# An LSTM scan on one core: every gate computed with the weights as the loaded operand

## What is computed

```python
def step(carry, xw_t):
    prev_h, prev_c = carry
    a = xw_t + prev_h @ Wh
    i = sigmoid(a[:, :H]); f = sigmoid(a[:, H:2*H]); o = sigmoid(a[:, 2*H:3*H]); g = tanh(a[:, 3*H:])
    next_c = f * prev_c + i * g
    next_h = o * tanh(next_c)
    return (next_h, next_c), next_h
# xW = x @ Wx + b, x is (2, 1024, 256); h0 = cond (2, 256), c0 = 0, H = 256
x = x + scan(step, (h0, c0), xW)          # 1024 steps, one after the other
x = x + ((x * (y * s)) @ weight) * rsqrt((y * s)**2 @ weight**2 + 1e-8)   # y = cond, s = 1/16
```

## Time and profile before

| | us |
|---|---|
| median of three runs (1942.17 to 1943.12) | 1943.04 |
| the profiled execution | 1940.92 |
| its span, from the first to the last instruction | 1939.1 |
| TensorE busy with matmuls / with loads | 1739.9 / 1577.4 |
| VectorE busy | 1263.6 |
| ScalarE busy | 886.4 |
| GpSimd busy | 258.1 |
| TensorE clock granted, mean share of 2.4 GHz | 0.996 |

### The profile page before, as it was taken

One profiled execution on the slowest core, in us unless ns is written; L12 is line 12 of the kernel. 1 busy time (PEld: TensorE's weight loads), 2 busy tenths in 40 slices (PEclk: granted clock), 3 DMA queues, 4 the chain that ended last, 5 costly groups with the idle time before them and its releaser, 6 DMA issues.

```text
span 1939.1 us, 303170 instructions
## 1 busy us (share of the span) xinstructions
PE 1739.9 (90%) x135928; PEld 1577.4 (81%) x135928; DVE 1263.6 (65%) x12825; ACT 886.4 (46%) x6148; POOL 258.1 (13%) x1295
## 2 busy tenths in 40 slices
PE   7989899999989898989999999889898989999998
PEld 7888888888888888888888888888888888888886
DVE  4666666666666666666666666666666666666665
ACT  2444444444444444444444444444444444444443
POOL 1111111111111111111111111111111111111110
PEclk8999999999999999999999999999999999999999
DMA  3000000000000000000000000000000000000001
GB/s 94 0 0 0 0 0 0 0 0 0 0 0 0 0 0 0 0 0 0 0 0 0 0 0 0 0 0 0 0 0 0 0 0 0 0 0 0 0 0 43
DMA packets 4444, 6.68 MB, mean 3 GB/s; under 512 B 1106, under 2 KB 2900, under 8 KB 4436
## 3 DMA queue, kind: packets, MB, share of 16 engines
q1 hardware_dynamic: 3872, 5.51, 0.9%
q10 hardware_dynamic: 564, 1.05, 0.2%
HBM read 4.46 MB, written 2.10 MB: 3 GB/s over the span
## 4 chain that ended last, share of the span: by engine, by line
PE 72%; ACT 15%; DVE 7%; issue 5%; DMA 0%; ACTq 0%
PE pA L221 24%; PE pS L235 15%; PE pB L235 14%; ACT tanhc L192 8%; ACT ogate L190 7%; DVE hst L384 7%; PE pA L228 6%; PE pA L207 6%; PE pA L201 6%; PE pA L322 1%; DMA bias_col<-in_bC_dram 0%; PE pB L213 0%; PE pS L313 0%; ACTq L173 0%; DVE ores L399 0%
## 5 line engine op out<-in xcount | busy, mean ns | idle before, releaser
L221 PE MATMUL pA<-wh_sb,hst 128*4 128x64 f32 (+2 forms) x24576 | 654.0, 220 | 180.0 <-DVE hst L384 177.9
L185 ACT ACTIVATE gates<-pB 128x8 f32<-128x8 f32 x2048 | 351.4, 184 | 1014.6 <-DVE pB L368 1006.1
L368 DVE STREAM_TRANSPOSE pB<-pA 128x64 f32<-128x64 f32 x2048 | 444.9, 263 | 449.4 <-PE pA L221 449.3
L221 PEld LDWEIGHTS pA<-wh_sb,hst 128*4 128x4 f32 (+2 forms) x24576 | 395.2, 87 | 295.4 <-DVE hst L384 292.8
L235 PE MATMUL pS<-hst,wh_sb 128*32 128x2 f32 x32768 | 509.7, 177 | 1.5 <-issue 1.5
L372 DVE CUSTOM_DVE_ANT_1 junk<-gates 128x4 f32<-128x4 f32 x4096 | 424.6, 160 | 113.8
L235 PE MATMUL pB<-hst,wh_sb 128*32 128x2 f32 x32768 | 465.0, 174 | 0.0
L235 PEld LDWEIGHTS pB<-hst,wh_sb 128*32 128x32 f32 x32768 | 430.6, 110 | 0.0
L143 POOL TENSOR_TENSOR xh<-xh,hst 128x4 f32 (+1 forms) x1024 | 206.9, 202 | 1652.1 <-DVE hst L384 1652.1
L235 PEld LDWEIGHTS pS<-hst,wh_sb 128*32 128x32 f32 x32768 | 423.9, 108 | 1.6 <-issue 1.6
L228 PE MATMUL pA<-wh_sb,hst 128*4 128x32 f32 (+3 forms) x16384 | 423.1, 193 | 0.0
(11 more groups left out here) (41 smaller groups left out, 295.5 us busy)
## 6 DMA issues: line engine op xcount, KB each, us to landing
outT_dram<-ores SPq DMA_DIRECT2D x8, 256.0 KB, 2.5
xh<-in_xT_dram SPq DMA_DIRECT2D x6, 320.0 KB
wh_sb<-in_Wh_dram ACTq DMA_DIRECT2D x1, 1024.0 KB, 8.1
wx_sb<-in_Wx_dram SPq DMA_DIRECT2D x1, 1024.0 KB, 7.6
w_sb<-in_w_dram SPq DMA_DIRECT2D x1, 256.0 KB, 6.7
xh<-in_xT_dram SPq DMA_DIRECT2D x2, 64.0 KB, 8.2
bias_sb<-in_bT_dram ACTq DMA_DIRECT2D x2, 1.0 KB
condT<-in_condT_dram ACTq DMA_DIRECT2D x1, 2.0 KB, 7.8
```

What stands on the lines that cost most here:

```text
L185: act.activation(gates[:, j, :, 0:2 * PAIR].rearrange("p b (q a) -> p a q b", a=PAIR), pB[:, j, :, 0:PAIR * Q].rearrange("p a (q r) -> p a ...
L221: last = pe.matmul(pA[j][c * Q:c * Q + M, 0:PAIR * Q].rearrange("p (g u) -> p g u", u=Q), hst[:, k, lo:lo + M], two(wh_sb[:, k, :], c, j, ...
L368: dve.transpose(pT[j][:, 0:PAIR * Q], pA[j][:, 0:PAIR * Q]).then_inc(turned_and_fsum_ready[j], 1)
```

## The change

- `turned`, `turned_one`, `two`, `fill_bias` and `fill_x` go, and with them the transposes of L368 and the bank `pA`. All four gates are computed with a 128x32 tile of the weights as the stationary operand (`add_h`): 48 matmuls for i, f and g and 16 for o in each step.
- h streams as `WIDE` = 16 columns, of which 14 are zeros: `hst` is laid out so that a window of 16 columns at `WIDE * t` has h at columns 2t and 2t+1. Each matmul adds to all 16 columns of its sum.
- i, f and g of one half lie side by side in one bank (`cells[j]`), and the sigmoid reads them there once TensorE is done with the half.
- All x sums go to banks of their own (`xcells`, `xouts`). `sum_x_cells(0)` (24 matmuls) runs in the first step of a body, `sum_x_cells(1)` (24) in the second, `sum_x_outs` (16) in the third. DVE carries them over with the bias in three additions, all in the first step of a body.
- `FILL` puts 1, 1, 2 and 1 fillers at the ends of the four steps.
- Step s of a body works on column pair t = (s + 3) % 4 where it was (s + 1) % 4, and `xp` is filled four time steps further ahead (`bodies`, POOL).

The diff, cut to its core:

```diff
-    TURNED = (I_, G_)
-    STILL = (F_, O_)
+    CELL_GATES = (I_, F_, G_)
+    NG = len(CELL_GATES)
     T = 4
     ROWS = T * B
+    WIDE = 16
+    LEAD = T - 1
     NBODY = SEQ // T
     CELL = 8
     AT_I, AT_F, AT_G, AT_HALF, AT_C = 0, 1, 2, 4, 5
     WARM = 32
-    AT_X = 256
+    FILL = (1, 1, 2, 1)
...
+        hst = sb("hst", [P, K, T * WIDE])
...
-        pA = [ctx.enter_context(nc.psum_tensor(f"pA{j}", [P, 512], F32)) for j in range(K)]
-        pB = ctx.enter_context(nc.psum_tensor("pB", [P, K, PAIR, 512], F32))
+        pG = ctx.enter_context(nc.psum_tensor("pG", [P, K, 512], F32))
         pS = ctx.enter_context(nc.psum_tensor("pS", [P, K, 512], F32))
-
-        pT = [pB[:, j, 0, :] for j in range(K)]
-        sums = [pB[:, j, 1, :] for j in range(K)] + [pS[:, j, :] for j in range(K)]
-        pD, pX, pO = pS[:, 0, :], pT[0][:, AT_X:AT_X + PAIR * K * ROWS], pA
+        pX = ctx.enter_context(nc.psum_tensor("pX", [P, K + 1, 512], F32))
+        pF = ctx.enter_context(nc.psum_tensor("pF", [P, 512], F32))
+        cells = [pG[:, j, 0:NG * WIDE].rearrange("p (n r) -> p n r", r=WIDE) for j in range(K)]
+        outs = [pS[:, j, 0:WIDE] for j in range(K)]
+        xcells = [pX[:, j, 0:NG * ROWS].rearrange("p (n r) -> p n r", r=ROWS) for j in range(K)]
+        xouts = pX[:, K, 0:K * ROWS].rearrange("p (j r) -> p j r", r=ROWS)
+        pD, pO = pS[:, 0, :], [pX[:, j, :] for j in range(K)]
...
         def h_slot(t):
-            return (ROWS + B) * t
+            return (WIDE + B) * t
...
+            for n in range(1, 3):
+                pool.wait_ge(x_summed, n)
+                spread(slice(n * T, (n + 1) * T))
...
-                        at = h_slot((s + 2) % T)
-                        now = xh[:, :, :, bass.ds(it * T + (s + 1), 1)]
-                        pool.tensor_tensor(now, now, hst[:, :, at:at + B].unsqueeze(3), ALU.add).then_inc(xh_ready, 1)
-                    pool.wait_ge(filled, it + 2)
-                    spread(bass.ds(it * T + 2 * T, T))
+                        if s == T - 1:
+                            pool.wait_ge(x_summed, it + 3)
+                            spread(bass.ds(it * T + 3 * T, T))
...
                 for s in range(T):
-                    t = (s + 1) % T
+                    t = (s + LEAD) % T
                     cols = slice(B * t, B * (t + 1))
                     for j in range(K):
-                        act.wait_ge(turned_and_fsum_ready[j], it * (2 * T) + 2 * (s + 1))
-                        act.activation(gates[:, j, :, 0:2 * PAIR].rearrange("p b (q a) -> p a q b", a=PAIR),
-                                       pB[:, j, :, 0:PAIR * Q].rearrange("p a (q r) -> p a q r", q=PAIR)[:, :, :, cols],
+                        act.wait_ge(sums_ready[j], it * T + (s + 1))
+                        act.activation(gates[:, j, :, 0:NG].rearrange("p b n -> p n b"), cells[j][:, :, cols],
                                        ACT.Sigmoid).then_inc(gates_ready[j], 1)
                     for j in range(K):
                         act.wait_ge(osum_ready[j], it * T + (s + 1))
-                        act.activation(ogate[:, j, :], sums[K + j][:, cols], ACT.Sigmoid)
+                        act.activation(ogate[:, j, :], outs[j][:, cols], ACT.Sigmoid)
...
-            def fill_bias(j):
+            def sum_x(to, j, g, k):
                 for c in range(G):
-                    last = pe.matmul(pA[j][c * Q:(c + 1) * Q, 0:PAIR * Q].rearrange("p (g u) -> p g u", u=Q), picks[:, :],
-                                     two(bias_sb[:, :], c, j, 1), start=True, stop=False, skip_group_check=True)
+                    last = pe.matmul(to[c * Q:(c + 1) * Q, :], tile(wx_sb[:, k, :], c, j, g), xp[:, k, :],
+                                     start=(k == 0), stop=(k == K - 1), skip_group_check=True)
                 return last
 
-            def fill_x(j, k):
+            def sum_x_cells(j):
+                for n, g in enumerate(CELL_GATES):
+                    for k in range(K):
+                        last = sum_x(xcells[j][:, n, :], j, g, k)
+                return last
+
+            def sum_x_outs():
+                for j in range(K):
+                    for k in range(K):
+                        last = sum_x(xouts[:, j, :], j, O_, k)
+                return last
+
+            def add_h(to, t, j, g, k, cs=range(G)):
+                for c in cs:
+                    last = pe.matmul(to[c * Q:(c + 1) * Q, :], tile(wh_sb[:, k, :], c, j, g),
+                                     hst[:, k, WIDE * t:WIDE * (t + 1)], start=False, stop=True, skip_group_check=True)
+                return last
+
+            def cell(t, j, n, k, cs=range(G)):
+                return add_h(cells[j][:, n, :], t, j, CELL_GATES[n], k, cs)
+
+            def clear(of):
                 for c in range(G):
-                    last = pe.matmul(pA[j][c * Q:c * Q + ROWS, 0:PAIR * Q].rearrange("p (g u) -> p g u", u=Q), xp[:, k, :],
-                                     two(wx_sb[:, k, :], c, j, G_), start=False, stop=False, skip_group_check=True)
...
-            def filler(start):
-                pe.matmul(pA[0][0:Q, P:2 * P], picks[:, :], zeros[:, :], start=start, stop=True, skip_group_check=True)
+                    pe.matmul(of[c * Q:(c + 1) * Q, :], picks[:, :], zeros[:, 0:of.shape[1]], start=True, stop=True)
+
+            def filler(count, start=False):
+                for _ in range(count):
+                    pe.matmul(pF[0:Q, 0:P], picks[:, :], zeros[:, :], start=start, stop=True, skip_group_check=True)
...
+            pe.wait_ge(operands_ready, 2)
+            for n in range(2):
+                pe.wait_ge(xp_ready, n + 1)
+                for j in range(K):
+                    if n:
+                        pe.wait_ge(x_carried[j], n)
+                    sum_x_cells(j)
+                if n:
+                    pe.wait_ge(x_carried[K], n)
+                sum_x_outs().then_inc(x_summed, 1)
             pe.wait_ge(operands_ready, 3)
...
+            early, late = range(G // 2), range(G // 2, G)
             with pe.Fori(0, NBODY) as it:
                 for s in range(T):
-                    t = (s + 1) % T
+                    t = (s + LEAD) % T
                     pe.wait_ge(h_ready[0], it * T + (s + 1))
-                    turned(t, 0, 0)
-                    turned_one(t, 1, 0, 0)
-
-                    pe.wait_ge(h_ready[1], it * T + (s + 1))
-                    turned(t, 0, 1).then_inc(sums_ready[0], 1)
-                    turned_one(t, 1, 0, 1)
-                    turned(t, 1, 1).then_inc(sums_ready[1], 1)
-                    if t == 0:
-                        pe.wait_ge(x_carried[0], it + 2)
-                    for j in range(K):
-                        still(t, F_, j, 0)
-                        still(t, F_, j, 1).then_inc(turned_and_fsum_ready[j], 1)
+                    for n in range(NG):
+                        cell(t, 0, n, 0)
                     if t == 0:
                         pe.wait_ge(x_carried[1], it + 2)
+                    cell(t, 1, 0, 0)
+                    cell(t, 1, 1, 0, early)
+
+                    pe.wait_ge(h_ready[1], it * T + (s + 1))
+                    for n in range(NG):
+                        last = cell(t, 0, n, 1)
+                    last.then_inc(sums_ready[0], 1)
+                    cell(t, 1, 1, 0, late)
+                    cell(t, 1, 2, 0)
+                    for n in range(NG):
+                        last = cell(t, 1, n, 1)
+                    last.then_inc(sums_ready[1], 1)
+                    if t == 0:
+                        pe.wait_ge(x_carried[K], it + 2)
                     for j in range(K):
-                        still(t, O_, j, 0)
-                        still(t, O_, j, 1).then_inc(osum_ready[j], 1)
-
-                    if s < PAIR:
-                        if s == 0:
-                            pe.wait_ge(xp_ready, it + 2)
-                        pe.wait_ge(gates_ready[0], it * T + (s + 1))
-                        for n, k in XSUMS[s * len(XSUMS) // PAIR:(s + 1) * len(XSUMS) // PAIR]:
-                            last = sum_x(n, k)
-                        if s == PAIR - 1:
-                            last.then_inc(x_summed, 1)
-                    elif t == T - 1:
-                        pe.wait_ge(gates_ready[1], it * T + (s + 1))
-                        for j in range(K):
-                            fill_bias(j)
-                        for j in range(K):
-                            for k in range(K):
-                                last = fill_x(j, k)
-                        last.then_inc(filled, 1)
+                        add_h(outs[j], t, j, O_, 0)
+                        add_h(outs[j], t, j, O_, 1).then_inc(osum_ready[j], 1)
+
+                    if s == 0:
+                        pe.wait_ge(xp_ready, it + 3)
+                        pe.wait_ge(x_carried[0], it + 2)
+                        sum_x_cells(0)
+                    elif s == 1:
```

(39 more changed lines are left out.)

111 lines of the change are left out of this document (31 added, 80 removed).

## The result

The changed kernel takes **1955.09 us** (median of 4 runs, 1953.64 to 1955.9) where the kernel before takes 1943.08 on the same chip: ratio 1.0061, 95% interval 1.0043 to 1.0078, 0.6% slower. The forecast was 1930, 0.7% faster. The time lies inside the stated range, but the change goes the other way than was forecast.

A forecast was written before the change was run, and what follows sets the result against it. TensorE, within a ring of engines per step, was taken as the bound. Steps 2.083 + 1.756 + 1.847 + 1.726 - 0.06 = 7.352 against 7.416; times 256 -16 us, start +3: 1943.04 - 13 = 1930 us, range 1862 to 2075.

The forecast's parts named there:

- The ring: Path from h through TensorE's sums, sigmoids, tanh and back to h in each step: 1.726 us, from 1.82 before.
- the slope: Sensitivity of the step to TensorE's pace per record: 1 ns of pace is some 0.1 us per step.
- the pace of a long run of alike records: 8.4 ns per TensorE record, read from 62 records with 8 columns and taken for the h sums.
- The fillers: Matmuls at the steps' ends on column tile 0, which the next step's first matmul needs: 0.216 us each.
- The first step: First step of a body, its x sums waiting for DVE's carry: 2.083 us, the wait costing 0.36.
- One wait hop less: Rival: the first step's x sums start 0.06 us after the carry, giving 1906 us; no separate chance given.
- Start-up: Head before the loop: two sets of 64 x matmuls instead of 56 in one, larger bodies to fetch: +3 us.
- DVE is never late: With transposes out of the ring, 0.32 us less there, DVE never delays a step.
- the rival of 2075: Rival: load and stream in series, or the o sums' pace for all, 10.1 ns; 2075 us, chance 0.18.
- The clock holds: Forecast counted on fillers to keep TensorE's clock up; rival of a falling clock: over 1990 us, chance 0.07.
- 27 ns for the increment: Upper bound for one semaphore increment in the o sums (13 taken): body 7.493, 1966 us.
- the fillers hold nobody: Rival: fillers delay no step, steps two and three 1.726, first 1.866: 1846 us; chance 0.17 together with quicker pace.

The follow-up runs named there:

- e1: Changed kernel with no fillers inside the loop (FILL all 0): 1882.85 us, ratio 0.9689 to the kernel before.
- e13: Changed kernel, its five loop fillers kept but each streaming 16 columns instead of 128: 1886.00 us, ratio 0.9711.
- e15: Changed kernel, fillers kept, the two x sets ahead as a loop of two rounds, carries' counts raised by one: 1968.94 us, ratio 1.0141.
- e9: Changed kernel without fillers, each x sum one step later, x sets ahead as a loop of two rounds, carries' counts raised by one: 1884.84 us.
- e3: Changed kernel, fillers kept, h streamed as 8 columns instead of 16: 1946.97 us, ratio 1.0026.
- e4: Changed kernel, fillers kept, each h matmul streaming only its 2 columns without zeros: 2815.73 us, ratio 1.4491.
- e11: e10 with the two x sets ahead as a loop of two rounds and the carries' counts raised by one: 1860.21 us, ratio 0.9582.
- e12: e11 with h streamed as 8 columns instead of 16: 1858.44 us, ratio 0.9566.
- e10: Changed kernel without fillers, x matmuls dealt out as 32 in the second step and 32 in the third: 1881.50 us, ratio 0.9687.
- e14: e10 with the carries' awaited count raised by one, the same number as for xp: 1864.59 us, ratio 0.9598.

## Why the prediction was wrong

The forecast body was 7.352, the measured one 7.433; by parts:

- **The ring, forecast 1.726, measured 1.770.** This is the term that turned the sign. Its part on TensorE was put at 95 x 8.4 + 13 ns = 0.811 from the first record to the last one of half 1's sum; measured it is 0.864, in every step that no filler holds, and the sigmoid starts at 1.10 (forecast 1.059). The 95 gaps are not alike: the first 34 records lie 7.9 apart but for 0.02 lost after the first four, 0.04 pass from the 34th to the 36th record, about where the wait for h of half 1 stands, the 24 records of half 0's sum have 8.7, and the 36 behind them 9.5. The other links are as forecast: 0.051 for the hop to ACT, then 0.16, 0.07, 0.23, 0.16 and 0.055. Three steps of a body carry the 0.044 in full: 0.13 a body, 34 us. I had named the slope (0.1 us a step for 1 ns of pace) and still took the pace of a long run of alike records for one that has a wait, an increment and a break in the order of column tiles inside (`early` ends on tile 1, and the next sum starts on tile 0). Which of these slows it stays open, but it is not h that is late: in e1's second step h of half 1 is there at 0.155, and the 37th record still starts at 0.316 (0.321 elsewhere).
- **The fillers, forecast 0.33 a body, measured 0.283** (e1). The size was near, the way was not. The forecast let a filler hold the whole of the next step. The trace shows that the first three records of the next step pass it (0.43, between the filler's two records at 0.37 and 0.48) and that later ones are held. The trace does not name column tiles; the filler writes tile 0, so the ones that are held should be tile 0's. The last record of half 1's sum starts at 0.995 in the second step (behind one filler), at 0.877 in the third (one) and at 0.962 in the fourth (two), instead of at 0.864. e13 shows that it is the 128 columns.
- **The first step, forecast 2.083, measured 1.866.** The carry came at 1.346 (forecast 1.304), but the hop after it was 0.054, not 0.15. That 0.15 exists: e15 has 0.16. What decides is not that there are two waits but, as far as the traces tell, whether one of them gets an instruction of its own. "One wait hop less" was a rival, and came true together with the slower ring. With both, and without its filler, the step is 1.84, the 1.85 that the forecast comes to without a filler: here the two errors cancel, which is luck.
- **Start-up, forecast +3, measured +9.** Some 5.7 of it lie ahead of the first h, and about half of the 9 is the fetching of code, at which TensorE stops seven times instead of four (see the result). In all ten profiles with the x sets as straight-line code it stops ahead of the second set's last two records, which start 2.1 to 2.7 us after the record before them (2.39 in the changed kernel); in the four with a loop that stop is missing. The other stop ahead of the first h (1.15 here) does not follow the loop: it comes in six of the ten and in two of the four, and just in those in which the first 16 KB transfer starts after 10.9 us; where it starts by 9.5, the code is there in time. Why it starts early or late is not shown. With all but the same code ahead of it the first h so comes anywhere from 18.0 to 20.6. The 4.3 to 4.8 of e9 and e15 are thus 2 to 3 from the loop, and the rest is mostly that neither has this stop. The remaining 3.7 are the first steps of the loop.
- Right: the transposes are off the path and DVE is never late in a plain step; 16 columns cost what 8 cost (e3), so load and stream don't add up, and the rival of 2075 is refuted, with the rule of the Trainium skill ("TensorE: Matmul & The Clock Gate", part 3) that a load overlaps matmuls only when the row group differs, for this case: all rows were in use in every matmul, and the records came 8 to 9.5 ns apart with 8 columns and with 16. (The same part of the Trainium skill also has loads for a background weight buffer go ahead, which would fit; the traces do not show which buffer a load goes to.) The clock holds, but with 16 columns it is the zeros that it needs (e4) and not the fillers (e1), on which the forecast had relied.

So the step that failed is the size of TensorE's part of the ring; the ring itself was the right path. By terms, in a body: +0.13 for the ring, -0.04 for the fillers, -0.01 for the first step, together 0.08, (7.433 - 7.352) x 256 = 21 us; with 6 more at the start, 1930 becomes 1957; measured 1955. One bound of the forecast does not follow from its terms: with 27 ns for the increment they give a body of 7.464 and 1959 us, not 7.493 and 1966; the measured time is inside either. The rival "the fillers hold nobody" (1846) fell with the fillers' 0.283; the changed kernel without them is at 1883. The change is worth 3.1% without its fillers, and 4.2% when in addition the x sums stand where nobody waits for them, the carries share xp's number and the x sets ahead are a loop (e11, 1860).

## What to carry to other kernels

- Work put in to keep the clock must be tried without: here, with h at 16 columns, it cost 72 us and kept nothing, while the zeros that rode beneath the loads cost about 8 us (16 columns against 8, e3) and the loop stayed at 1.00.
- In a loop whose steps are a ring, spare work goes where the engine is idle, and the idle time must be counted less the loop's branch (0.4 us from matmul to matmul) and less every number that the sequencer computes for a wait (0.1).
- A pace from one long run of alike records (8.4) is not the pace of a run with waits, increments and changes of tile order inside (9.1 on average); where the ring turns with it, take it from the nearest run that has them, and put the difference into the range.

## What was not expected of the hardware

- TensorE busy in 2762 of 2770 us and granted only 0.50 when h was 2 columns, 1.00 with 16 (and with 8, but for 20 us in e12, where the fillers were gone too).
- A 128-column matmul on one column tile does not hold all those behind it, by the code those on other tiles: the next step's first three records started 0.06 after the filler's first record and 0.05 ahead of its second (7.80, 7.86, 7.91).
- From the end of what is waited for to TensorE's matmul it is 0.05, or 0.15 to 0.16 where the sequencer has an instruction of its own for the wait (e15 and the kernel before); a register operation ahead of a wait costs 0.10 between matmuls that follow at once (e10) and nothing where TensorE waits anyway (the changed kernel). One number in one wait moved a kernel by 17 us (e10 to e14).
- Code that runs for the first time stops TensorE: seven times in the changed kernel, 12 us in all, each stop ending 2.3 to 2.9 us after the start of a 16 KB transfer on the instruction queue. Written as a loop of two rounds, the x sets ahead lost the longer of their two stops in all four kernels that had the loop.
